# Head attention with the value products split by halves of the keys, one half beside the other row half's scores, and each head's maximum taken in one reduction

## What is computed

```python
q = (src @ Wq).reshape(Bb, Tt, H, DH).transpose(0, 2, 1, 3)
k = (src @ Wk_c @ Wk).reshape(Bb, Tt, H, DH).transpose(0, 2, 1, 3)
v = (src @ Wv_c @ Wv).reshape(Bb, Tt, H, DH).transpose(0, 2, 1, 3)
q = _apply_rope(q, sin, cos)
k = _apply_rope(k, sin, cos)
attn = jnp.einsum('bhqd,bhkd->bhqk', q, k) / np.sqrt(DH)
attn = jax.nn.softmax(attn, axis=-1)
sa = jnp.einsum('bhqk,bhkd->bhqd', attn, v)
```

## Time and profile before

| | us |
|---|---|
| median of two runs | 1852.14 |
| the two runs | 1836.65 and 1867.64 |
| the profiled execution | 1841.07 |
| its span, first to last instruction | 1839.4 |
| TensorE busy | 1589.6 |
| VectorE busy | 1153.0 |
| ScalarE busy | 857.8 |
| GpSimd busy | 266.4 |

### The profile page before, as it was taken

How to read it: one execution, slowest core, us unless ns; L and a number is a source line. 1 busy time by engine, 2 the same in 40 slices (tenths; PEclk the granted TensorE clock), 3 DMA queues, 4 the chain that set the end, 5 groups by cost and what they waited for, 6 DMA issues and landing times. The chain is left out here.

```text
span 1839.4 us, 22955 instructions
## 1 busy us (share of the span) xinstructions
PE 1589.6 (86%) x8336; PEld 944.6 (51%) x8336; DVE 1153.0 (63%) x1612; ACT 857.8 (47%) x1572; POOL 266.4 (14%) x226
## 2 busy tenths in 40 slices
PE   7997949678888888888888888699999999999997
PEld 4554737422222222222222221288888888888886
DVE  4675526598888888888888881054646556374544
ACT  2444323127777777777777775331322313223130
POOL 1224900252300000000000000030211202121020
PEclk9998979759999999999999995589999999999999
DMA  6679662422422223333333310110101010010000
GB/s 205 233 267 340 165 165 101 69 73 65 92 49 47 45 50 47 50 53 53 53 53 53 53 47 12 57 41 13 46 12 57 6 51 34 23 57 0 24 1 23
DMA packets 95827, 132.73 MB, mean 72 GB/s; under 512 B 22896, under 2 KB 65792, under 8 KB 95744
## 3 DMA queue, kind: packets, MB, share of 16 engines
q1 hardware_dynamic: 85392, 107.51, 23.2%
q0 software_dynamic: 4496, 14.70, 3.2%
q10 hardware_dynamic: 5856, 9.44, 1.7%
HBM read 76.56 MB, written 54.53 MB: 71 GB/s over the span
## 5 line engine op out<-in xcount | busy, mean ns | idle before, releaser
L1113 DVE TENSOR_REDUCE h_halfmax<-h_sq 128x2 f32<-128x1024 f32 x512 | 604.0, 1219 | 138.8 <-PE h_sq L1018 137.4
L1083 ACT ACTIVATE h_p<-h_sk 128x512 f32<-128x512 f32 x1024 | 557.7, 595 | 262.3 <-PE h_sk L1038 241.8
L1400 PE MATMUL f_ob<-w_experts,f_h 128*128 128x512 f32 x1536 | 364.6, 396 | 0.0
L1038 PE MATMUL h_sk<-h_q,h_k 50*128 50x512 f32 x1024 | 242.3, 469 | 129.5 <-ACT h_p L1083 129.5
L1400 PEld LDWEIGHTS f_ob<-w_experts,f_h 128*128 128x128 f32 x1536 | 287.7, 188 | 66.7
L1051 PE MATMUL h_po<-h_p,h_v 128*32 128x512 f32 x2048 | 288.2, 637 | 0.0
L1018 PE MATMUL h_sq<-h_k,h_q 48*128 48x512 f32 x1024 | 245.5, 476 | 31.0 <-DVE h_halfmax L1113 23.1
L1038 PEld LDWEIGHTS h_sk<-h_q,h_k 50*128 50x128 f32 x1024 | 99.9, 192 | 266.7 <-ACT h_p L1083 263.9
L1018 PEld LDWEIGHTS h_sq<-h_k,h_q 48*128 48x128 f32 x1024 | 100.9, 194 | 262.7 <-issue 197.9
L1626 DVE SCALAR_TENSOR_TENSOR h_spare<-f_ob,f_wt,h_spare 128x256 f32<-128x256 f32 x128 | 61.8, 483 | 127.1 <-PE f_ob L1400 123.8
L1285 POOL TENSOR_TENSOR f_h<-h_spare,f_h 128x512 fp32r<-128x512 f32 x64 | 82.3, 1292 | 347.8 <-ACT f_h L1456 347.8
(11 more groups left out here) (163 smaller groups left out, 1449.7 us busy)
## 6 DMA issues: line engine op xcount, KB each, us to landing
h_q<-q_d SPq DMA_DIRECT2D x84, 128.0 KB, 5.9
h_k<-k_d SPq DMA_DIRECT2D x84, 128.0 KB, 6.8
ot_d<-h_o ACTq DMA_DIRECT2D x32, 256.0 KB, 3.8
q_d<-t_parts SPq DMA_DIRECT2D x12, 512.0 KB, 5.0
k_d<-t_parts SPq DMA_DIRECT2D x12, 512.0 KB, 5.2
p_xin<-in_L_attn_x SPq DMA_DIRECT2D x8, 512.0 KB, 5.1
xn_d<-p_xn SPq DMA_DIRECT2D x8, 512.0 KB, 3.8
xnT_d<-p_xnT SPq DMA_DIRECT2D x8, 512.0 KB, 5.8
```

The lines of the kernel that those rows point to most:

```text
L1038: ins = nc.tensor.matmul(sk[(f + g) % BANKS][:, :], k6[r][at, p, j * P:(j + 1) * P], q6[r][at, p, c * CH:(c + 1) * CH], start=True, stop=True)
L1083: nc.scalar.activation(probs[u % PR][:, h, :], sk[f % BANKS][:, :], ACT.Exp, scale=DH ** -0.5).then_inc(exp_done, 1)
L1113: nc.vector.tensor_reduce(halfmax[n % 2][:, m, :], sq[slot % 2][:, :, :], AX.X, ALU.max)\
L1400: ins = nc.tensor.matmul(to, h[left][:, KH * shared + k, at], weight, start=n == 0, stop=n == len(terms) - 1)
```

## The change

The scores of an item are now those of one head over all 1024 keys (two products on one row side), not of two heads over 512. `mix` is cut by keys: half 0 has the rows 0 to 63, half 1 the rows 64 to 127, each with four products of 64 rows and 32 columns, into a bank of its own (`h_po0`, `h_po1`). Half 0 is issued ahead of two scores and two query products that lie on rows 64 to 127, half 1 ahead of those on rows 0 to 63. The two banks are joined by ScalarE's copy and a new addition on VectorE (`add_out`), which now gives `out_taken`. `mix` runs two units behind the scores (`LAG`), `probs` has three buffers. The scores have two banks, one head each, and not three; in the last step, without items, they also take the four banks of `h_sq`. `larger` and `halfmax` are gone. The identity and the weight piece lie in buffers of the first chunk, which SyncE loads after the pieces are done. The core of the diff:

```diff
-        ITEMS = PAIRS * QT * NQ
+        ITEMS = GH * QT
-        BANKS = 3
+        BANKS = 2
-        PR = 2
+        PR = 3
+        LAG = 2
+        ORDER = (1, 3, 0, 2)
+        SIDE = [h % SIDES for h in ORDER]
+        spread_banks = [s[:, :] for s in sk] + [s[:, i, :] for s in sq for i in range(NQ)]
+        LAST = (STEPS - 1) * FILLS
+        bank_at = lambda f: f % BANKS if f < LAST else (f - LAST + LAST % BANKS) % len(spread_banks)
...
+                def queries(n, m, half):
+                    i, g, p = m // 2 % QT, SIDE[m % 2 * 2], m // (2 * QT)
...
+                    if half == 0:
+                        pe.wait_ge(sq_free[slot % 2], slot // 2)
+                    at = slice(g * SIDE_AT, g * SIDE_AT + DOTS)
+                    ins = nc.tensor.matmul(sq[slot % 2][:, half, :], q6[r][at, p, i * P:(i + 1) * P],
+                                           k6[r][at, p, half * CH:(half + 1) * CH], start=True, stop=True)
...
+                    if before[f] is not None:
+                        pe.wait_ge(exp_done, before[f] + 1)
+                    at = slice(h % SIDES * SIDE_AT, h % SIDES * SIDE_AT + ROWS)
+                    nc.tensor.matmul(spread_banks[bank_at(f)], k6[r][at, h // SIDES, j * P:(j + 1) * P],
...
                     for h in range(GH):
-                        ins = nc.tensor.matmul(po[h * VW:(h + 1) * VW, :], vh[n % RING][:, j, h, :],
-                                               probs[u % PR][:, h, :], start=j == 0, stop=j == QT - 1)
-                    ins.then_inc(pv_done, 1)
+                        ins = nc.tensor.matmul(po[half][h * VW:(h + 1) * VW, :], vh[n % RING][half_keys[half], j, h, :],
+                                               probs[u % PR][half_keys[half], h, :], start=j == 0, stop=j == QT - 1)
+                    if half == SIDES - 1:
+                        ins.then_inc(pv_done, 1)
...
+                    mixed = divmod(u - LAG, UNITS) if u >= LAG else None
+                    late = mixed and mixed[1] % QT == 0
+                    for b, coming in enumerate(ahead):
+                        if mixed and not late:
+                            mix(*mixed, b)
+                        if coming[1] == HELD and 0 < coming[0] <= STEPS:
+                            turn_maxima(coming[0] - 1)
+                        for i in range(NQ):
+                            if n < STEPS:
+                                score(n, w, b * NQ + i)
+                            if coming[0] < STEPS:
+                                queries(*coming, i)
+                    if late:
+                        for b in range(SIDES):
+                            mix(*mixed, b)
...
-                    nc.scalar.activation(outT[c][:, :], po[:, :], ACT.Copy).then_inc(out_taken, 1)
+                    nc.scalar.activation(outT[c][:, :], po[0][:, :], ACT.Copy).then_inc(half_taken, 1)
...
-                    nc.vector.tensor_reduce(halfmax[n % 2][:, m, :], sq[slot % 2][:, :, :], AX.X, ALU.max)\
-                        .then_inc(sq_free[slot % 2], 1)
+                    nc.vector.tensor_reduce(negm[n % 2][:, at:at + 1], sq[slot % 2][:, :, :].rearrange("p a b -> p (a b)"),
+                                            AX.X, ALU.max, negate=True).then_inc(sq_free[slot % 2], 1)
+                def add_out(n, c):
+                    dve.wait_ge(half_taken, n * NQ + c + 1)
+                    nc.vector.tensor_tensor(outT[c][:, :], po[1][:, :], outT[c][:, :], ALU.add).then_inc(out_taken, 1)
...
+                        unit, b = divmod((n - 1) * ITEMS + m - LEAD * PER, PER)
+                        done, behind = divmod(unit - LAG, QT)
+                        if b == 1 and behind == 0 and done > 0:
+                            add_out(*divmod(done - 1, NQ))
```

More of the change, by code:

```diff
@@ L999, in _ @@
                             sp.wait_ge(stored[c], (n - 1) * 16)
+                        sp.wait_ge(rests_done, len(ffw.pieces))
                         first_chunk.load_values(sp, 0, chunk_in)
@@ L1008, in _ @@
             def _(pe):
-                def item(n, m):
-                    p, i, half = m // (QT * NQ), m // NQ % QT, m % NQ
+                def queries(n, m, half):
+                    i, g, p = m // 2 % QT, SIDE[m % 2 * 2], m // (2 * QT)
                     r, slot = n % RING, item_slot(n, m)
-                    if m == 0 and n >= AHEAD:
+                    if m == 0 and half == 0 and n >= AHEAD:
                         pe.wait_ge(loaded[r], loads_of(n) if n % RING >= AHEAD else loads_of(n) - LOADS * 16)
[L1015 to L1020, removed]
+                    if half == 0:
[3 more added lines that the diff above has]
+                                           k6[r][at, p, half * CH:(half + 1) * CH], start=True, stop=True)
+                    if half == NQ - 1:
+                        ins.then_inc(sq_made, 1)
@@ L1030, in score @@
+                def score(n, w, i):
                     c, j = divmod(w, QT)
-                    r, f = n % RING, n * FILLS + w * GH + p * SIDES
-                    if w == 0 and p == 0:
+                    h = ORDER[i]
+                    r, f = n % RING, n * FILLS + w * GH + i
+                    if w == 0 and i == 0:
                         pe.wait_ge(shifted[r], shifts_of(n))
[L1034 to L1039, removed]
@@ L1055, in _, with both @@
+                    if half == SIDES - 1:
+                        ins.then_inc(pv_done, 1)
                 pe.wait_ge(const_set, 2)
+                def both(n, m):
+                    for half in range(NQ):
+                        queries(n, m, half)
                 for m in range(ITEMS):
-                    item(0, m)
+                    both(0, m)
                 for m in range(HELD):
-                    item(1, m)
+                    both(1, m)
                 turn_maxima(0)
                 for m in range(HELD, LEAD * PER):
-                    item(1, m)
@@ L1063, in _ @@
-                for u in range(STEPS * UNITS + 1):
+                    both(1, m)
+                for u in range(STEPS * UNITS + LAG):
                     n, w = divmod(u, UNITS)
                     ahead = [divmod(u * PER + ITEMS + LEAD * PER + b, ITEMS) for b in range(PER)]
-                    for p in range(PAIRS):
-                        if n < STEPS:
-                            score(n, w, p)
-                        if p == PAIRS - 1 and u:
-                            mix(*divmod(u - 1, UNITS))
-                        if ahead[p][0] < STEPS:
-                            item(*ahead[p])
-                    if ahead[-1] [1] == HELD - 1 and 0 < ahead[-1][0] <= STEPS:
-                        turn_maxima(ahead[-1][0] - 1)
+                    mixed = divmod(u - LAG, UNITS) if u >= LAG else None
[13 more added lines that the diff above has]
+                            mix(*mixed, b)
```

84 lines of the change are left out of this document (44 added, 40 removed).

## The result

The changed kernel takes 2985.33 us (median of two runs, 2985.17 and 2985.49). Against the kernel before it is 1.623 times the time (95% interval 1.615 to 1.631): slower, far past the range. Its profiled execution has a span of 2983.8 us, 1144 more than the 1839.4 before.

The account below looks back on a forecast made before the run. The prediction took a serial loop of 2.92 us a unit through TensorE and ScalarE as the bound. Units -9, last 20 units -29 and the stretch ahead +5 gave -33: 1841 - 33 = 1808 us, range 1775 to 2195.

Parts of the forecast that it names:

- Value products by row halves: Head attention: one half's value products overlap the other side's scores, so each row side needs 2.15 us a unit.
- Rival A: Each change of tile shape drains TensorE, all runs in series: 4.30 us a unit, 2188 us in all; chance 0.30.
- Rival C: The clock falls at the chunk's end, where TensorE stands about 2 us: +44 on the forecast, 1852 us; chance 0.04.
- The addition and who waits for it: VectorE's addition, 0.69 us, holds TensorE's value products at a chunk's end: about 3.5 us every 8 units.
- Two score banks: Scores with one head a bank: the bank loop sets 2.44 us a unit, replacing the 2.92.
- A head's maximum: VectorE's maximum of one head in one reduction: 1.14 us each stands, and dropping `larger` gains nothing.
- Ahead of the units: Stretch before the units, at half clock: a head's two products on one side, 40 items x 0.13, +5 us.
- The last 20 units: Last units, without items: six score banks let ScalarE's 1.98 us hold; 50 us taken for 79.1, -29 us.
- What bounds the kernel now: Middle units: scores, exponential, scores, value products, query products in series, 2.92 us a unit; no engine is full.

Follow-up runs that it names:

- A: TensorE alone, no waits, in the changed order: value products of one row half, then four 128-column products of the other; 2.12 us a half unit at full clock.
- K: TensorE alone in the changed order, but with everything on rows 0 to 63; 3.74 us a half unit, against 3.70 on different rows.
- B: TensorE alone, value products of both row halves next to each other; 20.8 us, the same as one row half alone with half the products.
- G: TensorE alone, four 128-column products of one side and then four of the other; 22.3 us for 192, 0.116 us a product.
- e7: The kernel before the change with two banks for the scores and not three, nothing else; 2125.43 us.
- the reordered kernel: The kernel before the change with TensorE's order edited: scores of the first pair, both items, scores of the second pair, value products; 1783.68 us, ratio 0.9665.
- the last kernel: The kernel before with both items between the two scores, and the last step's scores also in the four `h_sq` banks; 1753.31 us, ratio 0.9504.
- J: TensorE alone, one row half of the value products, then two pairs on both sides, begun at full clock; 1.65 us a repetition.
- e8: The kernel before with two score banks and split value products, plus 64 products over the whole array ahead of the first unit; 2687.22 us.
- e9: The changed kernel with both row halves of the value products together, plus 64 products over the whole array ahead of the first unit; 2488.05 us.

## Why the prediction was wrong, by its own steps

**Value products by row halves: the step that failed.** "The nearest rows are those in which four column strips and two row sides each run at once, so I take the overlap." Those rows had one shape each. The only rows of a *change* of shape were the late weight load at 704.26 and the 0.43 against 0.24, and both spoke for the drain; they were set aside because the forms shared rows. So a row side was priced at 2.15 us and the unit at 2.44; A, with the same products and no waits, takes 4.24 at full clock. Sharing rows does not matter: K on the same rows and A on different ones take the same time. The Trainium skill's rule (TensorEngine Tiling (Array Packing), Key Properties), that a change of tiling mode drains TensorE, and not a change of tile, is what A, B and G show. That tiles work independently, as it also says, held here within one mode only. Rival A had the right mechanism and its 4.30 us a unit was measured as 4.24.

**The clock: missing from rival A.** A's sum gives 2188 us; the other 797 are the half clock. Its unit was 4.30 and 1.3 / 8, so 4.46; measured were 7.59, and 3.13 x 236 = 739; its last 20 units were 67 us, measured 121. The sum of both is 793. The working kept the full clock in A and gave no reason. That TensorE would be busier than before is none, for busy time is no guide: TensorE's is 97% of the middle window at 0.50, where it was 82% at 0.99. Rival C put the only loss of clock within the 236 units at the chunk's end. The reading of what had held the clock was off too: it counts three pairs beside the value products in a unit, and the rows show four.

**The addition and who waits for it.** The place and the releaser are as told: 31 times, as the tile's view of the changed kernel says below. The 3.5 us for eight units were for the loop that overlaps; with all in series it is 57.8 / 31 = 1.9 us at half clock, where rival A said 1.3 at full. An addition took 0.68 us for the 0.69 forecast.

```profile
L1153 DVE TENSOR_TENSOR h_o<-h_po,h_o x32: 680/681/693, 468.8 to 2313.1; 128x512 f32<-128x512 f32 x32
```

```profile
its engine sat idle before it (us, times) until:
  DVE h_o L1153: 57.8, 31
```

**Two score banks.** 2.44 us a unit could not show in the changed kernel, where TensorE hides it. e7 shows that, with pairs, two banks cost 0.5 us a unit at full clock (3.43 for 2.92) and the steady clock besides; with one head a bank, as forecast, no run shows the 2.44. A cost on the clock was not in the prediction at all.

**A head's maximum.** Right: 1.224 us, in the group `L1147`. **Ahead of the units.** Right: 347.7 to 398.1 is 50.4 us for 45.9 before, +4.5 for the +5 forecast. **The last 20 units.** Forecast -29, measured +41. The spread of the scores is sound: where the clock holds, in the last kernel, a unit takes 1.96 us, ScalarE's 1.98 forecast. **What bounds the kernel now.** Right: the loop read from the earlier trace rows gave 2.7 us a unit and 1785 us for the reordered kernel ahead of its run, and 2.67 and 1783.68 came.

**The chances.** 0.30 for A was too little for the one case for which the trace had rows at changes of shape, and the upper bound of the range was A at full clock. By the last units of the kernel before, where the clock fell with TensorE busy 80% of the time, A at half clock was a case to price: with A's unit and last units doubled and its wait at the chunk's end kept, 8.6 + 0.16 us a unit, it is 1841 + 236 x 5.80 + 60 = 3270 us, and the 2985 would have lain inside.

## What to carry to other kernels

In every run here row and column tiles of TensorE ran side by side only while the tile shape stayed the same. A split that puts a second shape on the free half gains nothing, and it doubles the number of the products that it cuts (4096 records for 2048). How busy TensorE will be does not tell its clock, so price every new order at both levels, and try it alone, once begun at each level: a stretch that loses the full clock may never win it back. And where a chain of waits can be read off a timeline, first try the order that shortens it with the same instructions.

## What was not expected of the hardware

- The drain holds across disjoint rows: the other half's products began 1.00 us behind the value products at full clock (24.13 to 25.13), 1.87 at half (1003.62 to 1005.49).
- An order can hold a clock that it cannot reach: J's took 1.65 us a repetition when begun at full clock and 3.01 when begun at half, both with TensorE always busy.
- 64 products over the whole array (16.8 us) ahead of the units brought the full clock, and it was gone within 6 us of the first scores: behind two waits of 0.94 us in e8, with no gap between the products in e9.
- Value products of one row half take the time of both (20.8 us for 192 and for 384).
